# Bit-quantised feed-forward: which engine scales each tile, how the scales are made, and where tokens are rounded

## The chip, the core and the metric

The kernel runs on one core of a Trainium2 chip. A core has a matrix engine (TensorE, PE in the profile, with its weight loads as PEld), a vector engine (VectorE, DVE), an engine for activation functions (ScalarE, ACT), a general one (GpSimd, POOL) and a queue for transfers (SyncE, SP). Each runs its own list of instructions in order; semaphores tie them together. Matrix results land in PSUM, everything else lies in SBUF. The metric is the device time of one execution, in microseconds (us).

## The reference

Eight sequences of 256 tokens of width 256 pass through four pairs of attention and feed-forward, each added to its input. Only the last feed-forward is touched. It normalises each token, rounds tokens and weights to few levels, multiplies, convolves along the sequence, applies silu, rounds again and multiplies back:

```
def act_quant(x):
    scale = 127.0 / clip(max(abs(x), axis=-1), 1e-05)
    return clip(round(x * scale), -128, 127) / scale

h = bit_linear(x, w1)                       # 256 -> 1024
h = depthwise_conv1d(h, conv_w, conv_b)     # 3 taps along the tokens
h = silu(h)
out = bit_linear(h, w2)                     # 1024 -> 256
x = x + out
```

`bit_linear` applies `act_quant` to its input and multiplies by weights rounded to -1, 0, 1 times one scale.

## The kernel before

The program is a row of stages, one after the other; the last, `bit_ffn`, begins about 1534 us into the span and ends with it. It works on batches (sequences) of 256 tokens, held as two tiles of 128 tokens. The 1024 hidden channels are 8 channel tiles of 128 partitions by 256 tokens.

Every engine runs the same steps, 0 to 11; in step n five batches are in work, each in another phase (`new`, `turn`, `hid`, `end`, `last` for batches n, n-1, n-2, n-3, n-4):

- `new`: VectorE normalises the two token tiles (`xn`), finds each token's largest absolute value (`amax`, L2613) and makes two scales from it in four small operations (`token_scale`): `qs` = 127/max to round with, `qr` = max/127 to scale back. ScalarE rounds (`rounded`, L2718, into `q1`) by adding a large constant, `MAGIC`.
- `turn`: VectorE takes the constant off again and scales back (`unrounded`, L2632, into `q2`), TensorE turns the tokens (`turn_tokens`, into `px`), and they are split into a high part (ScalarE, L2725) and a low part (VectorE, L2637).
- `hid`: for each of 8 channel tiles TensorE makes the hidden values (`hidden`, L2808, one of three PSUM banks of `ph`), ScalarE does the middle tap with the bias (`middle_tap`, L2732), VectorE the first and the last tap (L2642, L2647), all into `y`. A bank is free again after the last tap, so the product of channel tile f waits for the last tap of tile f-3. After four channel tiles ScalarE applies silu to them (L2740, into `sT`).
- `end`: for each of two token tiles TensorE turns the activated values (`turn_silu`, L2819, into `pn`, one buffer), VectorE finds the largest of 1024 (L2656), makes two scales in four small operations (`tile_scale`: `saxc`, `srec`, `sqs`, `sqr`) and scales the tile (L2674, from `pn` into `s1`). GpSimd takes `MAGIC` off (`whole`, L2778, into `sq`), TensorE turns the tile back (`turn_back`, into `pb`).
- `last`: ScalarE copies `pb` out (`turned_back`, L2747, into `sqT`), TensorE multiplies (`product`, L2837, into `po`, one buffer), VectorE scales by `sqr` and adds to `x` (`residual`, L2681).

The order on each engine is written out by hand in its `step` function. On VectorE a step has 18 places, two per channel tile (even: first tap, odd: last tap) and two more, and other work is put in by place. On ScalarE and TensorE it goes by channel tile f. All waits are semaphores counted by batch. Steps 4 to 7 are a loop that holds two steps and runs twice; the other steps are written out. Steps 3 to 8 have all or nearly all phases in work and are called full here where all five are (4 to 7).

## Time and profile before

| | |
|---|---|
| median of 3 runs | 1703.01 us (1697.46 to 1704.25) |
| profiled execution, its own time | 1698.48 us |
| its span | 1696.6 us |
| granted TensorE clock, mean | 0.937 of full speed |
| busy share of the span | PE 86%, PEld 76%, DVE 57%, ACT 38%, POOL 25% |

The shares are means over all stages. This is the last part of the page's picture in 40 slices of 42.4 us each; the last four slices hold the stage that the change touches. Each digit is a tenth of the slice:

```profile
PE   4798997399986999999998799999999987875765
DVE  4576763312214666666665555555555547767996
ACT  1233333021213444444543244444444422234553
POOL 2011101134304443434332011010000026630212
```

Over the program TensorE is the busiest engine; in the last slices VectorE is. In a timeline row stand the start, the duration, engine, line, operation and what is written from what; a bracket gives the idle time before it and what ended it. The profile leaves out numbers in names: `f_q` is `q1` or `q2`, `f_s` is `s1`, `f_sq` is `sq`.

### The profile page before, as it was taken

Reading aid. Unit: us, or ns where it says so; the run is one execution under the profiler, and the core shown is the slowest. Engines: PE = TensorE matmul, PEld = TensorE weight load, DVE = VectorE, ACT = ScalarE, POOL = GpSimd, SP = SyncE. Lnnn points to the kernel's source line nnn. Section 1 sums busy time; section 2 is a strip of 40 time slices with the busy share of each in tenths; the row PEclk is TensorE's granted clock in tenths of the full one; section 3 lists DMA queues with packets and bytes.
Section 4 is the critical chain, followed back from the end, with each engine's and each line's share of the span. In section 5 each row is a group of like instructions: output and inputs, shape, how many; then the busy total and the mean of one; then the engine's idle time right before and its main releaser. Section 6 shows DMA issues by size and latency. Waiting matters only on the chain. (4 is left out here: it accounts for less than half of the span.)

```text
span 1696.6 us, 32771 instructions
## 1 busy us (share of the span) xinstructions
PE 1466.7 (86%) x11594; PEld 1282.5 (76%) x11594; DVE 971.6 (57%) x2432; ACT 638.5 (38%) x1414; POOL 420.6 (25%) x655
## 2 busy tenths in 40 slices
PE   4798997399986999999998799999999987875765
PEld 3466665389975788888887699999999976664554
DVE  4576763312214666666665555555555547767996
ACT  1233333021213444444543244444444422234553
POOL 2011101134304443434332011010000026630212
PEclk8699999599997999999999799999999999997898
DMA  7646430585410000010000444144338231100000
GB/s 149 114 79 112 77 52 14 203 277 180 133 41 29 8 8 20 14 36 20 1 8 14 165 171 157 41 174 175 120 109 294 69 94 47 35 7 1 14 12 26
DMA packets 97294, 139.83 MB, mean 82 GB/s; under 512 B 10080, under 2 KB 81248, under 8 KB 97056
## 3 DMA queue, kind: packets, MB, share of 16 engines
q1 hardware_dynamic: 79792, 109.83, 22.2%
q0 software_dynamic: 6368, 18.62, 3.9%
q10 hardware_dynamic: 11024, 9.97, 1.9%
q8 instruction: 63, 1.03, 0.3%
q14 instruction: 47, 0.39, 0.1%
HBM read 111.12 MB, written 14.42 MB: 74 GB/s over the span
## 5 line engine op out<-in xcount | busy, mean ns | idle before, releaser
L1872 PE MATMUL f_ph<-f_xgT,f_w 128*128 128x128 f32 x2496 | 287.0, 276 | 3.0 <-ACT f_xgT L1906 2.4
L1872 PEld LDWEIGHTS f_ph<-f_xgT,f_w 128*128 128x128 f32 x2496 | 283.8, 193 | 3.7 <-issue 1.9
L1031 ACT ACTIVATE a_work<-a_ps,a_bias 128x128 f32<-128x128 f32 (+1 forms) x256 | 104.1, 419 | 172.3 <-issue 90.7
L1953 DVE TENSOR_TENSOR f_w_low<-f_w,f_w_high 128x2048 fp32r<-128x2048 f32 x39 | 89.4, 2292 | 99.9 <-ACT f_w_high L1912 99.8
L1231 POOL TENSOR_TENSOR a_work<-a_work,a_recip 128x256 f32<-128x256 f32 (+1 forms) x128 | 103.2, 827 | 147.3 <-DVE a_recip L1150 146.3
L1843 POOL DMA_INDIRECT f_xg<-normed_x,order x38 | 36.0, 947 | 334.1 <-PE f_px L1861 325.6
L574 DVE CUSTOM_DVE_ANT_0 a_shut_s<-a_ps,a_neg 128x256 f32<-128x256 f32 x256 | 93.1, 420 | 41.5 <-PE a_ps L253 41.0
L486 ACT ACTIVATE a_pT<-a_ps 128x1024 f32<-128x1024 f32 x64 | 65.5, 1024 | 120.7 <-PE a_ps L253 120.7
L1912 ACT ACTIVATE f_w_high<-f_w 128x2048 fp32r<-128x2048 f32 x39 | 74.5, 1910 | 85.6 <-DVE f_yg L1965 85.6
L1155 DVE TENSOR_TENSOR a_qk<-a_ps,a_qk 128x512 fp32r<-128x512 f32 x64 | 44.3, 692 | 96.5 <-ACT a_qk L1048 96.5
L1674 PEld LDWEIGHTS f_ph<-f_xgT,f_w 128*128 128x128 f32 x736 | 87.8, 196 | 6.3 <-DMA f_w<-in_f_w 3.7
L1674 PE MATMUL f_ph<-f_xgT,f_w 128*128 128x128 f32 x736 | 88.9, 280 | 3.2 <-DMA f_w<-in_f_w 2.5
L1883 PE MATMUL f_py<-f_w_high,f_h_high 128*128 128x256 f32 x312 | 91.4, 293 | 0.0
L1883 PE MATMUL f_py<-f_w_high,f_h_low 128*128 128x256 f32 x312 | 88.1, 282 | 0.0
L1958 DVE TENSOR_TENSOR f_h_low<-f_raw,f_h_high 128x512 fp32r<-128x512 f32 x78 | 57.0, 730 | 54.3 <-ACT f_h_high L1916 54.3
L1883 PE MATMUL f_py<-f_w_low,f_h_high 128*128 128x256 f32 x312 | 88.0, 282 | 0.0
L1916 ACT ACTIVATE f_h_high<-f_raw 128x512 fp32r<-128x512 f32 x78 | 49.2, 631 | 91.8 <-DVE f_raw L1973 91.8
L1684 PE MATMUL f_py<-f_w,f_hT 128*128 128x256 f32 x368 | 83.5, 380 | 0.1
L1755 DVE TENSOR_SCALAR f_hT<-f_ph,f_b 128x128 f32<-128x128 f32 x92 | 25.9, 344 | 88.1 <-PE f_ph L1674 88.1
L1684 PEld LDWEIGHTS f_py<-f_w,f_hT 128*128 128x128 f32 x368 | 68.1, 190 | 9.1 <-issue 0.7
L1716 ACT ACTIVATE f_hT<-f_ph,f_b 128x128 f32<-128x128 f32 x92 | 26.2, 368 | 121.6 <-PE f_ph L1674 121.6
L1132 DVE TENSOR_REDUCE a_top_s<-a_ps 128x2 f32<-128x256 f32 (+1 forms) x128 | 64.2, 543 | 5.8 <-PE a_ps L917 5.8
(342 smaller groups left out, 3466.2 us busy)
## 6 DMA issues: line engine op xcount, KB each, us to landing
f_w<-in_f_w SPq DMA_DIRECT2D x70, 1024.0 KB, 7.3
sorted_y<-f_yg ACTq DMA_DIRECT2D x62, 128.0 KB, 1.7
a_qs<-a_part SPq DMA_DIRECT2D x48, 128.0 KB, 4.3
a_ks<-a_part SPq DMA_DIRECT2D x42, 128.0 KB, 6.2
normed_x<-a_xn SPq DMA_DIRECT2D x16, 256.0 KB, 2.2
x<-in_x SPq DMA_DIRECT2D x8, 256.0 KB, 6.6
a_mask<-in_mask SPq DMA_DIRECT2D x8, 256.0 KB, 6.4
a_maskT<-in_maskT SPq DMA_DIRECT2D x8, 256.0 KB, 6.5
```

The source lines that it names most:

```text
L486: act.activation(pT[:, u // 2 % 2, 2 * (u % 2):2 * (u % 2) + 2, :, :].rearrange("p j t n -> p j (t n)"), ps[:, ST:ST + 2, :], ACT.Exp, sca ...
L574: a = dve.tensor_tensor_reduce(out=shut_s[:, j, t, :], in0=ps[:, bank(m) + j, t * S:(t + 1) * S], in1=neg[:, m // U % 3, t, :], scale=1.0, ...
L1031: act.activation(prob[:, s, i, t * P:(P if t == 0 else TRI)], ps[:, SB + 2 * s + i, t * S:(t * S + P * (t + 1))], ACT.Exp, bias=bias[:, s, ...
L1132: dve.tensor_reduce(top_s[:, s, t, :], ps[:, SB + 2 * s:SB + 2 * s + 2, t * S:t * S + P * (t + 1)], AX.X, ALU.max).then_inc(max_done, 1)
L1231: pool.tensor_tensor(part, part, recip[:, s, t, :].unsqueeze(2).to_broadcast([P, 2, P * (t + 1)]), ALU.mult).then_inc(shares_done, 1)
L1674: mm = pe.matmul(ph[:, q, n, f * P:(f + 1) * P], w[:, s, k, (q * FQ + f) * P:(q * FQ + f + 1) * P], xgT[:, s, k, :], start=(k == 0), stop= ...
L1684: mm = pe.matmul(py[:, s, 0:D], hT[:, s, f, :], w2[:, s, f, :], start=(f == 0), stop=(f == FT - 1))
L1872: mm = pe.matmul(ph[:, q, n, f * P:(f + 1) * P], w[:, s, k, (q * FQ + f) * P:(q * FQ + f + 1) * P], xgT[:, s, k, :], start=(k == 0), stop= ...
L1883: mm = pe.matmul(py[:, s, 0:D], hT[a][:, s, f, :], w2_parts[b][:, s, f, :], start=(f == 0 and n == 0), stop=(f == FT - 1 and n == len(PASS ...
L1912: act.activation(w2_parts[0][:, s, :, :], w2[:, s, :, :], ACT.Copy).then_inc(w2_high, 1)
L1953: dve.tensor_tensor(w2_parts[1][:, s, :, :], w2[:, s, :, :], w2_parts[0][:, s, :, :], ALU.subtract).then_inc(w2_low, 1)
L1958: dve.tensor_tensor(hT[1][:, s, q * FQ:(q + 1) * FQ, :].rearrange("p f n -> p (f n)"), raw[:, q, :], hT[0][:, s, q * FQ:(q + 1) * FQ, :].r ...
```

## The change

Six edits, all in `bit_ffn`:

1. `token_scale` makes its two scales in two small operations: `qr` = max(amax, 1e-5) x 1/127 in one, `qs` = 1/`qr` in the next. The wait for `qr` in `unrounded` goes.
2. `tile_scale` likewise: `sunit` = max(sax, 1e-5) x 1/127, `sqs` = 1/`sunit`. The third, `sqr` = `sunit` x `unit` (the weights' scale), is made by GpSimd ahead of `whole`, with its own semaphore.
3. The first tile's scaling into `s1` is made by ScalarE (`scaled`), the second's by VectorE (`scaled_late`) at the end of the step.
4. ScalarE rounds the tokens after the middle tap of channel tile 7, ahead of the second silu, where it had done so at the step's end.
5. ScalarE's copy of the first turned tile (`turned_back`) moves from the end of a step to behind the middle tap 0 of the next; the copy of the second goes behind middle tap 3; the first silu goes behind middle tap 4.
6. TensorE's two products move from f = 2 and 4 to f = 4 and 5, VectorE's residuals from places 3 and 8 to 6 and 10.

The parts of the diff that carry these:

```diff
-                if k == 1:
-                    ins = dve.tensor_scalar(amaxc[:, :], amax[:, :], 1e-5, None, ALU.max)
-                if k == 2:
-                    ins = dve.reciprocal(rec[:, :], amaxc[:, :])
-                if k == 3:
-                    ins = dve.tensor_scalar(qs[:, :], rec[:, :], 127.0, None, ALU.mult)
-                if k == 4:
-                    ins = dve.tensor_scalar(qr[:, :], amaxc[:, :], 1.0 / 127.0, None, ALU.mult)
+                if k == 1:
+                    ins = dve.tensor_scalar(qr[:, :], amax[:, :], 1e-5, 1.0 / 127.0, ALU.max, ALU.mult)
+                if k == 2:
+                    ins = dve.reciprocal(qs[:, :], qr[:, :])
...
+            def scaled_late(pair, b):
+                i = TB * b + 1
+                dve.wait_ge(red_done, upto(pair, 3 * i + 2, 3 * TB))
+                if b >= 1:
+                    dve.wait_ge(sq_done, upto(pair, i - TB, TB))
+                dve.tensor_scalar(s1[:, 1, :], pn[:, :], sqs[:, 1:2], MAGIC, ALU.mult, ALU.add).then_inc(s1_done, 1)
...
+            def scaled(pair, b, t):
+                i = TB * b + t
+                act.wait_ge(red_done, upto(pair, 3 * i + 2, 3 * TB))
+                if i >= TB:
+                    act.wait_ge(sq_done, upto(pair, i - TB, TB))
+                act.activation(s1[:, t, :], pn[:, :], ACT.Identity, bias=magic[:, 0:1], scale=sqs[:, t:t + 1]
+                               ).then_inc(s1_done, 1)
...
+                pool.wait_ge(red_done, upto(pair, 3 * i + 1, 3 * TB))
+                if i >= TB:
+                    pool.wait_ge(resid_done, upto(pair, i - TB, TB))
+                pool.tensor_tensor(sqr[:, t:t + 1], sunit[:, t:t + 1], unit[:, 1:2], ALU.mult).then_inc(sqr_done, 1)
                 pool.wait_ge(s1_done, upto(pair, i, TB))
...
-                    if last and f == 2:
+                    if last and f == 4:
                         product(pair, n - 4, 0)
...
-                    if last and f == 4:
+                    if last and f == 5:
                         product(pair, n - 4, 1)
```

How the order moves is shown at three places; the names are as above, with the prefix `f3_`. First VectorE, the end of step 3, from the second tile's reduction to the next step. Before:

```order
L2656 TENSOR_REDUCE f3_sax<-f3_pn 128x1
L2619 RECIPROCAL f3_rec<-f3_amaxc 128x2
L2647 SCALAR_TENSOR_TENSOR f3_y<-f3_ph,t_cwu,f3_y 128x256
L2661 TENSOR_SCALAR f3_saxc<-f3_sax 128x1
L2642 SCALAR_TENSOR_TENSOR f3_y<-f3_ph,t_cwu,f3_y 128x256
L2663 RECIPROCAL f3_srec<-f3_saxc 128x1
L2621 TENSOR_SCALAR f3_qs<-f3_rec 128x2
L2647 SCALAR_TENSOR_TENSOR f3_y<-f3_ph,t_cwu,f3_y 128x256
L2665 TENSOR_SCALAR f3_sqs<-f3_srec 128x1
L2669 TENSOR_SCALAR f3_sqr<-f3_saxc,t_unit 128x1
L2623 TENSOR_SCALAR f3_qr<-f3_amaxc 128x2
L2674 TENSOR_SCALAR f3_s1<-f3_pn,f3_sqs 128x1024
```

And after:

```order
L2651 TENSOR_REDUCE f3_sax<-f3_pn 128x1
L2619 RECIPROCAL f3_qs<-f3_qr 128x2
L2642 SCALAR_TENSOR_TENSOR f3_y<-f3_ph,t_cwu,f3_y 128x256
L2658 TENSOR_SCALAR f3_sunit<-f3_sax 128x1
L2637 SCALAR_TENSOR_TENSOR f3_y<-f3_ph,t_cwu,f3_y 128x256
L2662 RECIPROCAL f3_sqs<-f3_sunit 128x1
L2642 SCALAR_TENSOR_TENSOR f3_y<-f3_ph,t_cwu,f3_y 128x256
L2669 TENSOR_SCALAR f3_s1<-f3_pn,f3_sqs 128x1024
```

Three small scalings between the last tap and the large scaling are gone, and so is one that stood ahead of the last tap; the scale `qs` for the tokens is ready two taps sooner. Taps are L2642 and L2647 before, L2637 and L2642 after.

Second ScalarE, all of step 3. Before:

```order
L2732 ACTIVATE f3_y<-f3_ph,t_fb,t_cwu 128x256 x4
L2725 ACTIVATE f3_xh<-f3_px 128x2x256
L2740 ACTIVATE f3_sT<-f3_y 128x1024
L2732 ACTIVATE f3_y<-f3_ph,t_fb,t_cwu 128x256 x4
L2740 ACTIVATE f3_sT<-f3_y 128x1024
L2747 ACTIVATE f3_sqT<-f3_pb 128x1024
L2718 ACTIVATE f3_q1<-f3_xn,f3_magic,f3_qs 128x256 x2
```

And after:

```order
L2728 ACTIVATE f3_y<-f3_ph,t_fb,t_cwu 128x256 x4
L2721 ACTIVATE f3_xh<-f3_px 128x2x256
L2728 ACTIVATE f3_y<-f3_ph,t_fb,t_cwu 128x256
L2743 ACTIVATE f3_s1<-f3_pn,f3_magic,f3_sqs 128x1024
L2736 ACTIVATE f3_sT<-f3_y 128x1024
L2728 ACTIVATE f3_y<-f3_ph,t_fb,t_cwu 128x256 x3
L2714 ACTIVATE f3_q1<-f3_xn,f3_magic,f3_qs 128x256 x2
L2736 ACTIVATE f3_sT<-f3_y 128x1024
```

The scaling (L2743) is new; one middle tap stands ahead of the first silu that stood behind it, and the rounding of the tokens stands ahead of the second silu.

Third TensorE, steps 10 and 11, the end of the program. Before:

```order
L2819 MATMUL f3_pn<-ident,f3_sT 128x128 x8
L2837 MATMUL f3_po<-t_w2q,f3_sqT 128x256 x8
L2828 MATMUL f3_pb<-identb,f3_sq 128x128 x8
L2837 MATMUL f3_po<-t_w2q,f3_sqT 128x256 x8
L2819 MATMUL f3_pn<-ident,f3_sT 128x128 x8
L2828 MATMUL f3_pb<-identb,f3_sq 128x128 x8
L2837 MATMUL f3_po<-t_w2q,f3_sqT 128x256 x8
L2828 MATMUL f3_pb<-identb,f3_sq 128x128 x8
L2837 MATMUL f3_po<-t_w2q,f3_sqT 128x256 x8
```

And after:

```order
L2831 MATMUL f3_pn<-ident,f3_sT 128x128 x8
L2840 MATMUL f3_pb<-identb,f3_sq 128x128 x8
L2849 MATMUL f3_po<-t_w2q,f3_sqT 128x256 x16
L2831 MATMUL f3_pn<-ident,f3_sT 128x128 x8
L2840 MATMUL f3_pb<-identb,f3_sq 128x128 x16
L2849 MATMUL f3_po<-t_w2q,f3_sqT 128x256 x16
```

The first tile's product stood between the turnings of the two tiles; now both turnings stand ahead of both products.

## Rows read from the trace of the kernel before

**Rows 1.** Stretch of step 6: us; busy PE, PEld, DVE, ACT, POOL; clock; DMA; GB/s.

```profile
1610.75:1627.77 17.02, 11.49 (x85) 9.73 (x83) 16.04 (x40) 9.28 (x16) 3.59 (x3) 0.90 0.04 15
```

**Rows 2.** Timeline of VectorE, last taps of steps 2, 3, 7, 9: start, duration.

```profile
1557.04 0.48 DVE L2647 SCALAR_TENSOR_TENSOR f_y<-f_ph,t_cwu,f_y 128x256 f32<-128x256 f32 x1
...
1572.44 0.47 DVE L2647 SCALAR_TENSOR_TENSOR f_y<-f_ph,t_cwu,f_y 128x256 f32<-128x256 f32 x1
...
1641.90 0.48 DVE L2647 SCALAR_TENSOR_TENSOR f_y<-f_ph,t_cwu,f_y 128x256 f32<-128x256 f32 x1
...
1672.63 0.48 DVE L2647 SCALAR_TENSOR_TENSOR f_y<-f_ph,t_cwu,f_y 128x256 f32<-128x256 f32 x1
```

**Rows 3.** Timeline of VectorE, around the start of step 6.

```profile
1607.94 0.14 DVE L2665 TENSOR_SCALAR f_sqs<-f_srec 128x1 f32<-128x1 f32 x1
...
1608.40 1.28 DVE L2674 TENSOR_SCALAR f_s<-f_pn,f_sqs 128x1024 f32<-128x1024 f32 x1
...
1610.75 1.05 DVE L2632 TENSOR_SCALAR f_q<-f_q,f_qr 128x256 f32<-128x256 f32 x1 [1.07 <-ACT f_q L2718]
...
1611.73 0.47 DVE L2642 SCALAR_TENSOR_TENSOR f_y<-f_ph,t_cwu,f_y 128x256 f32<-128x256 f32 x1
...
1612.12 0.34 DVE L2632 TENSOR_SCALAR f_q<-f_q,f_qr 128x256 f32<-128x256 f32 x1
...
1613.17 1.21 DVE L2656 TENSOR_REDUCE f_sax<-f_pn 128x1 f32<-128x1024 f32 x1
```

**Rows 4.** Timeline of ScalarE, around the start of step 6.

```profile
1608.06 1.06 ACT L2740 ACTIVATE f_sT<-f_y 128x1024 f32<-128x1024 f32 x1 [2.94 <-DVE f_y L2647]
...
1609.02 1.00 ACT L2747 ACTIVATE f_sqT<-f_pb 128x1024 bf16<-128x1024 bf16 x1
...
1609.92 1.08 ACT L2718 ACTIVATE f_q<-f_xn,f_magic,f_qs 128x256 f32<-128x256 f32 x2
...
1610.91 1.00 ACT L2732 ACTIVATE f_y<-f_ph,t_fb,t_cwu 128x256 f32<-128x256 f32 x2
```

**Rows 5.** Timeline of GpSimd, first tile of step 3 and second tile of step 5.

```profile
1567.66 1.90 POOL L2778 TENSOR_TENSOR f_sq<-f_s,f_magic 128x1024 bf16<-128x1024 f32 x1 [48.60 <-DVE f_s L2674]
...
1609.77 1.89 POOL L2778 TENSOR_TENSOR f_sq<-f_s,f_magic 128x1024 bf16<-128x1024 f32 x1 [5.40 <-DVE f_s L2674]
```

**Rows 6.** Timeline of VectorE, a small scaling in step 3.

```profile
1569.32 0.26 DVE L2617 TENSOR_SCALAR f_amaxc<-f_amax 128x2 f32<-128x2 f32 x1
```

**Rows 7.** Timeline of VectorE, tap 3 and tap 5 of step 6.

```profile
1616.43 0.47 DVE L2642 SCALAR_TENSOR_TENSOR f_y<-f_ph,t_cwu,f_y 128x256 f32<-128x256 f32 x1
...
1621.22 0.47 DVE L2642 SCALAR_TENSOR_TENSOR f_y<-f_ph,t_cwu,f_y 128x256 f32<-128x256 f32 x1
```

**Rows 8.** Timeline of ScalarE, the copy of turned tokens in step 6.

```profile
1616.14 0.60 ACT L2725 ACTIVATE f_xh<-f_px 128x512 fp32r<-128x512 f32 x1
```

**Rows 9.** Timeline of ScalarE, the table load in step 2.

```profile
1550.35 1.28 ACT L2740 ACT_TABLE_LOAD   x1
```

**Rows 10.** Timeline of VectorE, tap 4 and tap 5 of step 2.

```profile
1553.19 0.48 DVE L2642 SCALAR_TENSOR_TENSOR f_y<-f_ph,t_cwu,f_y 128x256 f32<-128x256 f32 x1 [1.51 <-ACT f_y L2732]
...
1554.70 0.48 DVE L2642 SCALAR_TENSOR_TENSOR f_y<-f_ph,t_cwu,f_y 128x256 f32<-128x256 f32 x1
```

**Rows 11.** Timeline of TensorE, turning of an activated tile, first and second of step 6.

```profile
1609.74 1.76 PE L2819 MATMUL f_pn<-ident,f_sT 128*128 128x128 f32 x8 [0.92 <-DVE f_s L2674]
...
1619.59 1.09 PE L2819 MATMUL f_pn<-ident,f_sT 128*128 128x128 f32 x8 [1.73 <-DVE f_s L2674]
```

**Rows 12.** Timeline of TensorE, the end of the program.

```profile
1687.60 1.03 PE L2828 MATMUL f_pb<-identb,f_sq 128*128 128x128 bf16 x8 [1.21 <-POOL f_sq L2778]
...
1689.74 1.89 PE L2837 MATMUL f_po<-t_w2q,f_sqT 128*128 128x256 bf16 x8 [1.12 <-ACT f_sqT L2747]
```

**Rows 13.** Timeline of VectorE, the last instruction.

```profile
1691.67 0.48 DVE L2681 SCALAR_TENSOR_TENSOR x<-f_po,f_sqr,x 128x256 f32<-128x256 f32 x1 [4.76 <-PE f_po L2837]
```

**Rows 14.** Timeline of GpSimd, a small product in an earlier stage.

```profile
1518.03 0.19 POOL L2137 TENSOR_TENSOR m_square<-m_guess 128x2 f32<-128x2 f32 x1
```

More of the change, by code:

```diff
@@ L2530, in bit_ffn @@
         xn, q1, q2 = (sb(n, [P, TB, D]) for n in ("xn", "q1", "q2"))
-        amax, amaxc, rec, qs, qr = (sb(n, [P, TB]) for n in ("amax", "amaxc", "rec", "qs", "qr"))
+        amax, qs, qr = (sb(n, [P, TB]) for n in ("amax", "qs", "qr"))
         xh, xl = (sb(n, [P, 2, DK, S + 2], F32R) for n in ("xh", "xl"))
@@ L2534, in bit_ffn @@
         sT = sb("sT", [P, 2, FT, S])
-        sax, saxc, srec, sqs, sqr = (sb(n, [P, TB]) for n in ("sax", "saxc", "srec", "sqs", "sqr"))
+        sax, sunit, sqs, sqr = (sb(n, [P, TB]) for n in ("sax", "sunit", "sqs", "sqr"))
         s1, sq = sb("s1", [P, TB, F]), sb("sq", [P, TB, F], BF16)
@@ L2630, in unrounded @@
                     dve.wait_ge(x_turned, upto(pair, b - 1))
-                dve.wait_ge(prep, upto(pair, 5 * b + 4, 5))
                 dve.tensor_scalar(q2[:, t, :], q1[:, t, :], MAGIC, qr[:, t:t + 1], ALU.subtract, ALU.mult
@@ L2686, in step @@
                 new, turn, hid, end, last = (is_batch(n - i) for i in range(5))
-                for place in range(2 * FT + 2):
+                for place in range(2 * FT + 1):
                     if turn and place < TB:
                         unrounded(pair, n - 1, place)
-                    if end and 3 <= place < 9:
+                    if end and 3 <= place < 6:
                         tile_scale(pair, n - 3, 0, place - 3)
@@ L2693, in step @@
                         (first_tap, last_tap)[place % 2](pair, n - 2, place // 2)
-                    if end and place >= 12:
+                    if end and 12 <= place < 15:
                         tile_scale(pair, n - 3, 1, place - 12)
-                    if last and place in (3, 8):
-                        residual(pair, n - 4, (3, 8).index(place))
+                    if end and place == 2 * FT:
+                        scaled_late(pair, n - 3)
+                    if last and place in (6, 10):
+                        residual(pair, n - 4, (6, 10).index(place))
                     if new and place in (5, 6):
@@ L2701, in step @@
                         low_part(pair, n - 1)
-                    if new and place in (9, 10, 12, 14, 16):
-                        token_scale(pair, n, (9, 10, 12, 14, 16).index(place))
+                    if new and place in (9, 10, 12):
+                        token_scale(pair, n, (9, 10, 12).index(place))
             every_step(dve, step)
@@ L2714, in rounded @@
                 for t in range(TB):
-                    act.wait_ge(prep, upto(pair, 5 * b + 3, 5))
+                    act.wait_ge(prep, upto(pair, 3 * b + 2, 3))
                     if b >= 1:
@@ L2751, in step @@
                 for f in range(FT):
+                    if hid:
+                        middle_tap(pair, n - 2, f)
+                    if last and f == 0:
+                        turned_back(pair, n - 4, 0)
                     if last and f == 3:
                         turned_back(pair, n - 4, 1)
-                    if hid:
-                        middle_tap(pair, n - 2, f)
                     if turn and f == 3:
                         high_part(pair, n - 1)
-                    if hid and f % 4 == 3:
-                        silu(pair, n - 2, f // 4)
-                    if end and f == 7:
-                        turned_back(pair, n - 3, 0)
-                if new:
-                    rounded(pair, n)
+                    if end and f == 4:
+                        scaled(pair, n - 3, 0)
+                    if hid and f == 4:
+                        silu(pair, n - 2, 0)
+                    if new and f == 7:
+                        rounded(pair, n)
+                    if hid and f == 7:
+                        silu(pair, n - 2, 1)
             every_step(act, step)
```

28 lines of the change are left out of this document (10 added, 18 removed).

## Prediction

> **What bounds the kernel now.** I read the view of stretches over the last stage first. In one full step (step 6) VectorE is busy 16.04 us of 17.02, TensorE 11.49 at a granted clock of 0.90, ScalarE 9.28, GpSimd 3.59 [rows 1]. So only in this stage, and in it only VectorE, is there no slack; the edits touch no other stage. Then I read VectorE's timeline to get the length of the steps, from the start of the last tap of one to that of the next: step 3 takes 15.40 us, steps 4 to 7 take 69.46 us (17.37 each), steps 8 and 9 together 30.73 us [rows 2]. Steps 10 and 11 are a chain that passes from engine to engine; the last instruction begins 19.04 us after the last tap of step 9 [rows 2, 13].
>
> Third, the start of a step. VectorE does three small scalings (0.46 us from the first to the large scaling), the large scaling `f_s` (1.28 us), waits 1.07 us for ScalarE's rounded tokens, and then its first `f_q` takes 1.05 us, where the same operation takes 0.34 us a little later [rows 3]. ScalarE is late with the tokens because it does silu and the copy of turned tiles first, 1608.06 to 1609.92 [rows 4]. The long `f_q` ends at 1611.80; GpSimd's `f_sq` ran from 1609.77 to 1611.66 [rows 3, 5]: VectorE was held until GpSimd was done.
>
> Of two neighbours on VectorE the second starts 0.08 us before the first one's end (1611.73 with 0.47, next 1612.12 [rows 3]). So a tap costs 0.39, a small scaling of 0.14 costs 0.06, the large scaling 1.19.
>
> **The change, part by part.**
>
> Start of a step, in us from where the three small scalings began (1607.94). Before, the next reduction starts at 5.23 [rows 3]. After, the small scalings are gone or stand earlier, so the large scaling runs 0 to 1.19 and its result is there at 1.28. The tokens are rounded already; the first `f_q` takes 0.26, to 1.45. The first tap needs ScalarE's bias tap, which now stands directly behind silu: silu from 0.12 (1608.06), the next 0.96 later (1609.02), bias tap about 0.56, so ready at 1.64 [rows 4]; tap 0 starts at 1.69. The second `f_q` would start at 2.08, but GpSimd's `f_sq` starts 0.09 after the large scaling (1609.77 against 1609.68), at 1.37, and runs 1.89, to 3.26 [rows 3, 5]. The `f_q` then frees VectorE at about 3.33. Two more taps: the reduction starts at 4.11. Gain 1.12. The hold is still there, it only moved from the first `f_q` to the second; without it the bias tap of channel tile 1 (behind the 1.00 us copy [rows 4], ready at 3.02) would be the limit and the reduction would start at 3.46, 0.65 earlier.
>
> The Trainium skill (SBUF — State Buffer, "SBUF: two separate sides") says that GpSimd and VectorE's two-port operations share a pair of ports as an exclusive lock: who starts first keeps it for the whole instruction. The trace agrees with the 1.05 against 0.34 us. The same page would count every `tensor_scalar` between SBUF tiles, the small ones too; that is the rival "held twice" below.
>
> Rest of a full step. The first tile's large scaling leaves VectorE: 1.19. Two small scalings of that tile and one of the tokens go: 0.06 to 0.13 each, 0.2 together. Gain 1.4. What it costs ScalarE: no row shows this scaling there; by the nearest rows it is 1.06 (silu, same size [rows 4]) to 1.28 (VectorE's own [rows 3]); I take 1.15, nearer the ScalarE row. ScalarE has 17.0 - 9.3 = 7.7 us free [rows 1], so the total is no problem, but the place is: between bias tap 3 and bias tap 5 ScalarE now has the copy 1.00, the token copy 0.60 [rows 8], two bias taps of 0.56, the scaling 1.15 and silu 1.06, less five overlaps of 0.1: 4.4 us. VectorE needs from tap 3 to tap 5 4.79 us now [rows 7], less 1.19 and a small one: 3.5 us. ScalarE's lead at tap 3, 0.7 to 1.3 us by my schedule, covers most. I put the wait at 0.3 us per step (bounds 0 and 1.0).
>
> GpSimd gets one product of one column per tile, 0.19 us by a row of another stage [rows 14]. It stands ahead of `f_sq` and waits for the residual of the same buffer. The residual comes at place 6 of a step, before ScalarE's scaling ends, so in full steps it costs nothing; behind it waits only `f_sq`, and TensorE's turn back at the step's end, over 3 us later.
>
> TensorE's two products move two and one places back, behind the turn back of the second tile. Tap 3 needs the hidden product 3, which stands behind the turned tokens (held `f_q`, 3.4) and the turn back of a tile that GpSimd ends at 3.26; both are needed anyway. Cost 0 in full steps. At half clock TensorE's group takes 1.76 instead of 1.09 [rows 11]; that is inside the 0.3.
>
> So a full step saves 1.12 + 1.4 - 0.3 = 2.2 us; four of them 8.8.
>
> Step 3: no `f_sq` runs at its start. The two roundings (1.08, less 0.1 [rows 4]) no longer stand ahead of bias tap 0: 0.9; rest as above 1.4. Together 2.3.
>
> Steps 8 and 9: step 8 starts like a full step (1.1), step 9 rounds no tokens and gains only the small scalings (0.5); the rest 1.4 each. VectorE has no norms and fewer other things between tap 3 and tap 5 here, so it waits more for ScalarE: 0.6 each. Together 3.2.
>
> Steps 0 to 2: in step 2 silu's table load of 1.28 us [rows 9] stood ahead of bias tap 4, and VectorE waited 1.51 us; tap 5 started at 1554.70 [rows 10]. Now the load comes behind bias tap 4 (ScalarE free from about 1550.70): load to 1551.98, silu to 1552.95, bias tap 5 ready 1553.5. Gain 1.1. Two small operations less in the tokens' chain of steps 0 and 1: 0.3. Together 1.4.
>
> Steps 10 and 11: at the end TensorE turned the last tile back (1687.60, 1.03 us), waited for ScalarE's copy, did one product (1.89) and the residual followed at 1691.67 [rows 12, 13], 3.04 us after the turning. Now both products stand behind this turning, and the second one waits for the first one's residual: 1.89 + 0.48 + 1.89 and three hand-overs of 0.1: 4.5 us. Loss 1.5. Against it stand two dependent small operations less for each of two tiles (0.2 each, 0.8) and the earlier start of the step (0.4). Net loss 0.3.
>
> Sum: -1.4 - 2.3 - 8.8 - 3.2 + 0.3 = -15.4 us. The profiled execution took 1698.48 us (span 1696.6), so it would take 1683.1; it lies 4.5 under the median of the runs, 1703.01. Off the median: 1687.6. I forecast 1687.5.
>
> **The rivals.**
>
> Everything meets: no wait for ScalarE (0.3 x 4 and 0.6 x 2 back), tail even, and the hold falls away in part because GpSimd's new small product delays `f_sq` past the second `f_q` (0.65 x 5). That is 2.4 + 0.3 + 3.2 = 5.9 more: 1681.5. Against it: the small product's inputs are ready long before, so it delays nothing.
>
> Held twice: at the loop's ends VectorE may reach the first `f_q` after GpSimd's start, and the tokens' small scaling at place 10 may meet the first tile's `f_sq`. A small scaling took 0.26 us at 1569.32, to 1569.58, where `f_sq` ended at 1569.56 [rows 5, 6], so small ones are held too. By my schedule `f_sq` of the first tile ends 0.8 us before that place; with ScalarE a microsecond late it doesn't, and up to 1.3 us per step in six steps go: 7.8. Time 1695.5.
>
> Nothing comes of it: another wait fills what VectorE gives up, ScalarE's queue above all. At its upper bound (1.0 per full step instead of 0.3, and 2 in steps 8 and 9) plus held twice: about 3 + 3 + 7.8 back of 15.4: 1701.5.
>
> Slower, by TensorE's clock: if the moved waits keep it at its lower level (1.2 GHz) through the steps, its 11.49 us [rows 1] grow by the 1.76 / 1.09 of rows 11 to 18.5, and with the 0.9 us in which it waits for the large scaling [rows 11] a step takes 19.4, 2.0 more than the 17.37. It then bounds the stage: 5 steps, +10, time 1713. It decides once more than about three quarters of each step run at the lower level. Against it: 0.90 was granted, and in a shorter step its gaps shrink.
>
> **How the numbers follow.** Under 0.5% (8.5 us) is what a measurement of this kernel can't tell from no change. Forecast 0.60 (own range 1683 to 1692), everything meets 0.12, held twice 0.18, nothing 0.07, slower 0.03. The range leaves out the last two and little of the others: 1677 to 1697. Faster (below 1694.5): 0.60 + 0.12 + two thirds of 0.18 = 0.84; same: a third of 0.18 and the 0.07 = 0.13; slower 0.03.
>
> **What would show it.** The distance of last taps in full steps near 15.1 us; no wait of VectorE for `f_q`; a second, not a first, `f_q` of 1.2 us or more; the new ScalarE scaling 1.06 to 1.28 us; tap 5 of a full step waiting 0 to 0.5 us for ScalarE; step 2 without the 1.51 us wait at tap 4; some 4.5 us between the last turn back and the last residual. Wrong: VectorE waiting over 1 us per step for bias taps, small scalings of 0.3 us or more at place 10, or a granted clock well under 0.9 in full steps.

## The result, and the profile after

| | before | after |
|---|---|---|
| median, run side by side on one chip | 1701.48 us (1697.46 to 1704.78) | 1683.70 us (1677.31 to 1688.16) |
| ratio, after to before | | 0.9905, 95% interval 0.9882 to 0.9928 |
| profiled execution, its own time | 1698.48 us | 1677.31 us |
| its span | 1696.6 us | 1675.4 us |
| granted TensorE clock, mean | 0.937 | 0.945 |

Faster by 0.95%, 17.8 us between the medians. 1687.5 was forecast, with 1677 to 1697 as the range. Of the 21.2 us between the spans, 4.5 are not the change: the stage's first instruction starts at 1534.26 us before and at 1529.74 after, and nothing ahead of it was edited (in the kernels of the experiments below, whose earlier stages are the same too, it lies between 1528.90 and 1543.99). From there to the start of the last residual the stage took 157.41 us and takes 140.69: 16.7 less, where the prediction's sum was 15.4. "Stage" below is always this stretch, which leaves out what the rest of the program does.

The view of stretches over steps 4 to 7, each from the start of the last tap of one step to that of the next (length, then busy time of PE, PEld, DVE, ACT, POOL, then granted clock, share of the DMA engines' time, GB/s), first two of the four of before:

```profile
1572.44:1589.97 17.53, 12.87 (x85) 10.90 (x84) 16.07 (x43) 9.39 (x15) 3.79 (x2) 0.79 0.05 16
...
1624.68:1641.90 17.22, 11.50 (x86) 9.85 (x85) 16.24 (x42) 9.39 (x15) 3.79 (x2) 0.90 0.05 15
```

and of after:

```profile
1564.07:1578.81 14.74, 11.15 (x85) 10.06 (x84) 14.58 (x34) 10.43 (x17) 4.31 (x4) 0.86 0.06 19
1578.81:1593.56 14.75, 11.13 (x87) 9.95 (x87) 14.59 (x35) 10.53 (x17) 4.24 (x4) 0.90 0.06 19
1593.56:1608.67 15.11, 11.56 (x86) 10.20 (x85) 14.66 (x34) 10.49 (x17) 4.31 (x4) 0.89 0.05 18
1608.67:1623.42 14.75, 10.95 (x86) 9.88 (x85) 14.59 (x35) 10.51 (x17) 4.24 (x4) 0.88 0.05 18
```

VectorE is still the engine without slack (14.59 of 14.75), ScalarE took over a scaling of 1.2 us per step, and the steps lie near the 15.1 that was forecast.

The start of step 5 after, which answers to [rows 3 to 5]. VectorE:

```profile
1579.21 1.27 DVE L2669 TENSOR_SCALAR f_s<-f_pn,f_sqs 128x1024 f32<-128x1024 f32 x1
1580.41 0.34 DVE L2627 TENSOR_SCALAR f_q<-f_q,f_qr 128x256 f32<-128x256 f32 x1
1580.88 0.48 DVE L2637 SCALAR_TENSOR_TENSOR f_y<-f_ph,t_cwu,f_y 128x256 f32<-128x256 f32 x1
1581.28 1.37 DVE L2627 TENSOR_SCALAR f_q<-f_q,f_qr 128x256 f32<-128x256 f32 x1
...
1583.36 1.21 DVE L2651 TENSOR_REDUCE f_sax<-f_pn 128x1 f32<-128x1024 f32 x1
```

GpSimd and then ScalarE (its first copy, and later in the step the new scaling):

```profile
1580.57 1.93 POOL L2790 TENSOR_TENSOR f_sq<-f_s,f_magic 128x1024 bf16<-128x1024 f32 x1 [1.83 <-DVE f_s L2669]
```

```profile
1580.75 1.01 ACT L2751 ACTIVATE f_sqT<-f_pb 128x1024 bf16<-128x1024 bf16 x1
...
1586.68 1.23 ACT L2743 ACTIVATE f_s<-f_pn,f_magic,f_sqs 128x1024 f32<-128x1024 f32 x1
```

The first `f_q` is short and nothing waits for it; the second is held: it ends at 1582.65, just behind the end of `f_sq` at 1582.50. The hold moved from one to the other, as forecast. The wait of 1.51 us at tap 4 of step 2 [rows 10] is gone; what is left there is this, at tap 5:

```profile
1548.67 0.48 DVE L2637 SCALAR_TENSOR_TENSOR f_y<-f_ph,t_cwu,f_y 128x256 f32<-128x256 f32 x1 [0.47 <-ACT f_y L2728]
```

The end of the program, which answers to [rows 12, 13]. TensorE, then VectorE's last residual:

```profile
1665.12 1.03 PE L2840 MATMUL f_pb<-identb,f_sq 128*128 128x128 bf16 x8 [3.83 <-POOL f_sq L2790]
1665.94 1.91 PE L2849 MATMUL f_po<-t_w2q,f_sqT 128*128 128x256 bf16 x8
1668.53 1.87 PE L2849 MATMUL f_po<-t_w2q,f_sqT 128*128 128x256 bf16 x8 [0.67 <-DVE x L2675]
```

```profile
1670.43 0.48 DVE L2675 SCALAR_TENSOR_TENSOR x<-f_po,f_sqr,x 128x256 f32<-128x256 f32 x1 [2.05 <-PE f_po L2849]
```

From the end of the last turning back (1666.15) to the last residual it is 4.28 us, where 4.5 was forecast and it was 3.04 before.

### The profile page after: what moved, and what is told of

The parts are those of the page before. It is cut to its first block and busy times, and to the rows that moved or that the text cites. A ratio compares the mean times of both kernels' runs of the same rounds, so it can differ in the third digit from the quotient of the medians.

```text
span 1675.4 us, 32751 instructions
## 1 busy us (share of the span) xinstructions
PE 1453.5 (87%) x11594; PEld 1275.4 (76%) x11594; DVE 960.2 (57%) x2376; ACT 648.3 (39%) x1422; POOL 424.8 (25%) x671
```

## The experiments

Twelve kernels ran. A ratio is always to the kernel before, and has an interval of 3 to 6 us on each side, so most of what is said of parts rests on the stage and on single steps of one profiled execution each. All times are us; the clock of a step is the mean that the view of stretches shows for it.

| kernel | ratio (interval) | stage | steps 0-2 | 3 | 4-7 | 8 | 9 | rest |
|---|---|---|---|---|---|---|---|---|
| before | 1 | 157.41 | 22.78 | 15.40 | 69.46 | 16.35 | 14.38 | 19.04 |
| after | .9905 (.9882-.9928) | 140.69 | 21.27 | 13.06 | 59.35 | 14.18 | 14.14 | 18.69 |
| 1 scaling back on VectorE | .9929 (.9904-.9953) | 147.41 | 21.16 | 14.81 | 63.73 | 14.84 | 13.83 | 19.04 |
| 2 rounding behind silu | .9922 (.9905-.9938) | 144.28 | 21.31 | 13.96 | 61.43 | 14.81 | 14.14 | 18.63 |
| 3 four small operations | .9918 (.9896-.9940) | 149.38 | 21.01 | 13.61 | 63.58 | 15.97 | 15.57 | 19.64 |
| 4 unroundings ahead | .9936 (.9916-.9956) | 148.18 | 20.83 | 13.12 | 64.97 | 16.47 | 14.15 | 18.64 |
| 5 unroundings back to back | .9917 (.9884-.9950) | 143.52 | 20.83 | 13.12 | 62.35 | 14.55 | 13.33 | 19.34 |
| 6 late copy | .9883 (.9856-.9911) | 141.29 | 21.31 | 13.13 | 59.43 | 14.34 | 14.74 | 18.34 |
| 7 ahead and late copy | .9906 (.9870-.9941) | 140.90 | 20.81 | 13.13 | 60.90 | 14.13 | 13.63 | 18.30 |
| 8 both products back | .9969 (.9947-.9992) | 152.79 | 21.31 | 13.12 | 67.43 | 16.89 | 16.54 | 17.50 |
| 9 first product early at the end | .9904 (.9882-.9927) | 142.43 | 21.13 | 13.00 | 60.58 | 14.78 | 13.36 | 19.58 |
| 10 first product back | .9935 (.9912-.9958) | 146.27 | 21.30 | 13.06 | 62.66 | 16.38 | 14.17 | 18.70 |
| 11 unroundings around the scaling | .9898 (.9874-.9921) | 142.13 | 20.83 | 13.13 | 60.45 | 15.33 | 13.66 | 18.73 |
| 12 = 11 + 6 + 9 | .9889 (.9862-.9915) | 136.49 | 20.83 | 13.13 | 58.73 | 13.92 | 13.63 | 16.25 |

**1. The first tile's scaling back on VectorE.**

```diff
+                    if end and place == 8:
+                        scaled_first(pair, n - 3)
...
-                    if end and f == 4:
-                        scaled(pair, n - 3, 0)
```

The added lines are VectorE's, the ones taken out ScalarE's.

> The changed kernel with one edit undone: the first tile's scaling stands on VectorE again, at place 8 of a step (where it was before), not on ScalarE. Measured on the stage alone, from its first instruction (the memset of the constant) to the start of the last residual: 157.41 us before, 140.69 us after. Theory (VectorE's queue is the bound, each microsecond taken from it is gained): the scaling comes back as 1.19 us in each of steps 3 to 9, 8.3 us, less the waits for ScalarE that the changed kernel has in steps 6, 8 and 9 (0.3, 0.7 and 2.4 us, of which half goes): stage about 147 us, ratio to before about 0.994. Rival (ScalarE's copy was paid in ScalarE's queue, so moving it back costs nothing): stage within 1 us of 140.7.

Stage 147.41. All four full steps took 15.93 or 15.94 at a clock of 0.88 to 0.90, 1.18 more than the 14.75 of after, which is the 1.19 that the scaling costs in VectorE's queue. The step that answers to [rows 1]:

```profile
1586.39:1602.32 15.93, 11.44 (x87) 9.96 (x86) 15.77 (x36) 9.52 (x16) 4.24 (x4) 0.90 0.05 18
```

**2. The rounding behind the second silu again.**

```diff
-                    if new and f == 7:
-                        rounded(pair, n)
                     if hid and f == 7:
                         silu(pair, n - 2, 1)
+                    if new and f == 7:
+                        rounded(pair, n)
```

> The changed kernel with one edit undone: ScalarE rounds the tokens at the end of a step again, behind the second silu. Theory (the rounding is needed for the first unrounding, and it delays the bias tap 0 behind it, but most of that is hidden because GpSimd holds VectorE anyway): the first unrounding, not the second, is held until GpSimd's work ends (over 1 us), and the first reduction of a full step starts 0.5 to 0.9 us later; over steps 3 to 8 the stage becomes 4 to 5 us longer, 145 us. Rival (the whole wait of 1 us and the held time of 1 us come back beside each other, 2 us a step): 151 us or more.

Full steps of 15.35 or 15.36, 0.61 more than in after. The hold and the wait are on the first `f_q` again, as before the change:

```profile
1607.38 1.59 DVE L2627 TENSOR_SCALAR f_q<-f_q,f_qr 128x256 f32<-128x256 f32 x1 [0.53 <-ACT f_q L2714]
```

**3. Four small operations per scale, none on GpSimd.**

```diff
-                    ins = dve.tensor_scalar(qr[:, :], amax[:, :], 1e-5, 1.0 / 127.0, ALU.max, ALU.mult)
-                if k == 2:
-                    ins = dve.reciprocal(qs[:, :], qr[:, :])
+                    ins = dve.tensor_scalar(amaxc[:, :], amax[:, :], 1e-5, None, ALU.max)
+                if k == 2:
+                    ins = dve.reciprocal(rec[:, :], amaxc[:, :])
...
```

Two more operations follow, and `tile_scale` is undone likewise.

> The changed kernel with the small operations undone: four small operations for each scale on VectorE as before (the third scale also on VectorE, none on GpSimd), all else as changed. Theory: five small operations more in a full step at 0.06 to 0.13 us, of which two or three stand bare between last tap and large scaling where each costs 0.15: 0.6 to 0.7 us a step, and 0.4 us in each dependent chain of steps 0, 1, 10 and 11: stage 140.7 + 4.5 + 1.6 = 146.8 us. Rival (small operations vanish in the gaps between taps that wait for each other anyway): stage below 142.5 us.

149.38, 2.6 over what was expected. The stretches tell the two parts apart:

```profile
1592.09:1608.38 16.29, 12.76 (x86) 11.32 (x85) 15.64 (x41) 10.37 (x17) 3.79 (x2) 0.79 0.06 18
...
1624.79:1640.15 15.36, 11.06 (x85) 9.99 (x85) 15.29 (x41) 10.39 (x17) 3.79 (x2) 0.89 0.05 17
```

The two steps at a clock of 0.89 take 15.52 and 15.36, 0.6 to 0.8 over after: the small operations. The two at 0.79 take 0.9 more, with 1.5 us more of busy TensorE. In full steps the small operations are worth what was said; that the rest is TensorE at its lower level more of the time is read from these rows, and no run isolates it. In steps 0 and 1 they cost the 0.4 too (12.20 us from the start of the stage to tap 0 of step 2, against 11.79 in after), but step 2 was 0.67 shorter than in after, so the column of steps 0 to 2 doesn't show it.

**4. Both unroundings ahead of the late scaling,** so that neither meets `f_sq`.

```diff
-                    if turn and place < TB:
-                        unrounded(pair, n - 1, place)
...
+                    if new and place == 2 * FT:
+                        for t in range(TB):
+                            unrounded(pair, n, t)
                     if end and place == 2 * FT:
                         scaled_late(pair, n - 3)
```

> The changed kernel with the two unroundings of a step's tokens moved from places 0 and 1 of the next step to ahead of the late large scaling, so that they are done before GpSimd starts on that tile. Theory (an operation of VectorE between SBUF tiles is held while GpSimd computes, 1.37 us instead of 0.34 in steps 4 to 8): both take 0.34 us, the large scaling comes 0.5 us later, tap 0 follows it at once, and the reduction is then bound by TensorE's turning of the tile: a full step gets 0.5 to 1.1 us shorter, the stage 3 to 5 us, 136 to 138 us. Rival (the long duration is something of the instruction itself or of its input's arrival, not of GpSimd): the second unrounding stays long wherever it stands, stage 140 us or more.

A miss, by 10 to 12 us. The hold was gone (both unroundings together took 0.61), and VectorE's busy time fell to 13.93 per step, but the steps grew:

```profile
1587.77:1603.33 15.56, 11.40 (x86) 10.10 (x85) 13.93 (x34) 10.50 (x17) 4.21 (x4) 0.89 0.06 18
1603.33:1619.58 16.25, 12.73 (x86) 11.20 (x85) 13.94 (x35) 10.51 (x17) 4.27 (x4) 0.79 0.05 17
```

The late scaling started 0.93 after the last tap instead of 0.40, and TensorE waited for it:

```profile
1590.12 1.94 PE L2832 MATMUL f_pn<-ident,f_sT 128*128 128x128 f32 x8 [1.06 <-DVE f_s L2669]
```

From this came a new theory. Beside VectorE's queue runs a second chain: late scaling, turning of the next tile, hidden products 2 and 3 with the turned tokens and a turn back between, middle taps, copies, ScalarE's scaling, silu, middle tap 5. In the changed kernel it is nearly as long as the queue.

**5. Both unroundings back to back behind the late scaling.**

```diff
-                    if turn and place < TB:
-                        unrounded(pair, n - 1, place)
+                    if turn and place == 0:
+                        for t in range(TB):
+                            unrounded(pair, n - 1, t)
```

> The changed kernel with the two unroundings standing one behind the other at place 0, directly behind the late large scaling; before, tap 0 stood between them. It asks who gets the way to SBUF that VectorE and GpSimd hold against each other. GpSimd's work starts 0.17 us after the first unrounding, the second would start 0.26 after it. Theory (it goes to who asks first, and GpSimd asks between the two): the second is held, 1.4 us as now, but ahead of tap 0, which then can't use the time; the first reduction of a full step starts 0.3 to 0.4 us later, the stage is 142 to 143 us. Rival (VectorE keeps it while its next operation wants it too): both take 0.34, VectorE gets 1 us free per full step, of which the chain through ScalarE lets some 0.3 through: 138 to 139.5 us.

Stage 143.52, 0.5 over what was expected, and one of the four full steps took 16.56 where the others took 15.26; the hold stays. The two, now one row, took 2.25 us, to 1590.05; `f_sq` had begun 0.16 after the first of them and ended at 1589.89. VectorE, then GpSimd:

```profile
1587.80 2.25 DVE L2627 TENSOR_SCALAR f_q<-f_q,f_qr 128x256 f32<-128x256 f32 x2
```

```profile
1587.96 1.93 POOL L2791 TENSOR_TENSOR f_sq<-f_s,f_magic 128x1024 bf16<-128x1024 f32 x1 [1.84 <-DVE f_s L2669]
```

Being next in VectorE's queue doesn't keep the port: GpSimd takes it between two neighbours.

**6. ScalarE's second copy out of the second chain.**

```diff
-                    if last and f == 3:
+                    if last and f == 5:
                         turned_back(pair, n - 4, 1)
...
-                    if last and f == 5:
+                    if last and f == 7:
                         product(pair, n - 4, 1)
...
-                    if last and place in (6, 10):
+                    if last and place in (6, 15):
```

> The changed kernel with ScalarE's copy of the second turned tile moved from behind bias tap 3 to behind bias tap 5, its product from f = 5 to 7, its residual from place 10 to 15. That takes 0.9 us out of the chain late scaling, turning of the tile, hidden products 2 and 3, bias tap 3, copies, bias tap 4, scaling, silu, bias tap 5. Theory (in the changed kernel VectorE's queue is the bound and this chain is slack by 0 to 0.5 us in steps 4, 5 and 7): only the waits at tap 5 go (0.3 in step 6, 0.7 in step 8, 1.5 in step 9): stage 138 to 139.5 us. Rival (the chain is the bound already): 0.9 us in each of steps 4 to 8, stage 135 us or less.

Full steps as in after (59.43 against 59.35), so in the changed kernel VectorE's queue is the longer one, and the gain looked for in steps 8 and 9 didn't come: a miss in size.

**7. Experiments 4 and 6 together.**

> Both moves together: the unroundings ahead of the late scaling (stage 148.2 us by itself, 7.5 more than the changed kernel, although nothing is held) and ScalarE's second copy behind bias tap 5. Theory (the first move made the chain that begins with the late scaling 0.5 us later and so the bound; the trace shows VectorE waiting at taps 3 and 5): with 0.9 us out of the chain the loss goes and the gain of the free unroundings shows: full steps of 14.2 to 14.8 us, stage 136 to 140 us. Rival (moving the unroundings costs by itself, by TensorE's clock or by the tokens' turning): stage 146 us or more also with the second move.

Stage 140.90, near the 136 to 140 of the theory, where 4 alone had 148.18. But the steps don't bear the theory out at like clock: at 0.79 a full step took 16.32 (in 4: 16.25 to 16.61), at 0.89 it took 15.79 (in 4: 15.56), with VectorE waiting 1.12 us at tap 3. The gain lies in the two full steps at a clock of 1.00, and experiment 4 has none of those. Steps 4, 5 and 7 of experiment 7 (step 4 has no transfers out yet and one instruction of GpSimd less):

```profile
1562.84:1579.16 16.32, 12.66 (x86) 11.17 (x85) 13.76 (x33) 10.51 (x17) 4.07 (x3) 0.79 0.01 2
1579.16:1593.44 14.28, 9.96 (x86) 8.60 (x85) 13.84 (x35) 10.30 (x16) 4.24 (x4) 1.00 0.06 20
...
1607.95:1623.74 15.79, 11.37 (x86) 10.12 (x85) 13.99 (x34) 10.48 (x17) 4.24 (x4) 0.89 0.05 17
```

So it isn't shown that the late copy by itself makes up for the later start; what is shown is that with it the loss is gone in the steps in which TensorE kept its upper level. The late copy may bring that about: the three kernels that have it (6, 7, 12) ran 6 of their 12 full steps at 1.00, the other eleven 1 of 44. Each is a single profiled execution, and why it is so stays open. Open is also the size in experiment 4: at like clock (0.89 against 0.90) its step is 0.8 us longer than in after, for a start only 0.53 later, while the turning took 1.94 us instead of 1.55.

**8. Both products and residuals where they stood before** (edit 6 alone undone).

```diff
-                    if last and f == 4:
+                    if last and f == 2:
                         product(pair, n - 4, 0)
...
-                    if last and f == 5:
+                    if last and f == 4:
                         product(pair, n - 4, 1)
...
-                    if last and place in (6, 10):
+                    if last and place in (3, 8):
```

> The changed kernel with TensorE's products back at f = 2 and 4 and VectorE's residuals at places 3 and 8. Theory: in steps 10 and 11 the first product stands between the two turnings again, so from the last turning to the last residual it takes 3.0 us instead of 5.3: 1.5 to 2.3 us less; in full steps the first product stands ahead of hidden product 2 and 3, in the chain that is nearly the bound, at up to 1.6 us: it adds 0.3 to 1 us to each of steps 4 to 9. Stage 141 to 145 us. Rival (products are free wherever they stand): 138.5 to 139.2 us, only the end changes.

The tail fell by 1.2, where 1.5 to 2.3 was expected. The full steps grew by 2.0 each instead of 0.3 to 1, a miss of nearly 8 us in the stage, and it is the slowest version: ratio 0.9969. Of the 16.7 us only 4.6 are left without edit 6. The clock isn't it (0.90 in all four full steps; two of them):

```profile
1565.47:1582.08 16.61, 11.43 (x86) 9.80 (x85) 14.76 (x35) 10.54 (x17) 4.20 (x4) 0.90 0.05 17
1582.08:1599.00 16.92, 11.41 (x87) 9.83 (x85) 14.90 (x34) 10.67 (x17) 4.20 (x4) 0.90 0.05 17
```

TensorE waits for ScalarE's copy ahead of the second product, with hidden product 4 queued behind it, and VectorE then waits for middle tap 4:

```profile
1589.19 0.56 ACT L2728 ACTIVATE f_y<-f_ph,t_fb,t_cwu 128x256 f32<-128x256 f32 x1 [0.84 <-PE f_ph L2820]
1589.65 1.01 ACT L2751 ACTIVATE f_sqT<-f_pb 128x1024 bf16<-128x1024 bf16 x1
```

```profile
1590.72 1.05 PE L2849 MATMUL f_po<-t_w2q,f_sqT 128*128 128x256 bf16 x8 [1.57 <-ACT f_sqT L2751]
```

```profile
1592.96 0.48 DVE L2637 SCALAR_TENSOR_TENSOR f_y<-f_ph,t_cwu,f_y 128x256 f32<-128x256 f32 x1 [1.08 <-ACT f_y L2728]
```

This isn't the order of the kernel before. There ScalarE's copy stood ahead of middle tap 3, and edit 5 moved it behind; TensorE then waited 0.58 us for it, and VectorE nowhere for middle tap 4 (step 6 of before, ScalarE and TensorE):

```profile
1614.78 1.02 ACT L2747 ACTIVATE f_sqT<-f_pb 128x1024 bf16<-128x1024 bf16 x1 [0.32 <-PE f_pb L2828]
1615.70 0.56 ACT L2732 ACTIVATE f_y<-f_ph,t_fb,t_cwu 128x256 f32<-128x256 f32 x1
```

```profile
1615.86 1.05 PE L2837 MATMUL f_po<-t_w2q,f_sqT 128*128 128x256 bf16 x8 [0.58 <-ACT f_sqT L2747]
```

So experiment 8 shows what the products' old places cost beside the copies' new ones. No run has both old, and how the 2.0 us divide between the later copy and the shorter queue of VectorE stays open.

**9. The first product at f = 2 in steps 10 and 11 alone.**

```diff
-                    if last and f == 4:
+                    if last and f == (4 if hid else 2):
                         product(pair, n - 4, 0)
```

> The changed kernel, with TensorE's product of the first tile at f = 2 again in the steps without a hidden phase (10 and 11) and nothing else. Theory: at the end of the program the first product and its residual then run while GpSimd still has the last tile, so one product (1.89 us) and one residual fewer stand behind the last turning back: tail 18.69 -> 17.5 us (the run with both products moved back showed 17.50), every step before it unchanged, stage 140.7 -> 139.5. Rival: the residual's hand-over, not the product, sets the end; then the tail stays within 0.3 of 18.7.

A miss: 19.58 instead of 17.5. From the end of the last turning back to the last residual it is 3.05 again instead of 4.28, as said. But in step 10 the product, 1.91 at TensorE's lower level, now stands ahead of a turning back, its copy and the turning of the next tile; from one turning of a tile to the next it took 7.30 us (1662.70 to 1670.00) instead of 5.52 (1653.56 to 1659.08). The order isn't all of it: experiment 8 has TensorE's same order in steps 10 and 11 and took 17.50 there, at a clock of 0.86 and with residuals at earlier places; this one had 0.69, and after 0.73. Up to step 9 this kernel issues what after does, and still one step took 1.3 us more:

```profile
1586.90:1601.64 14.74, 9.90 (x86) 8.65 (x85) 14.58 (x34) 10.50 (x17) 4.24 (x4) 1.00 0.06 19
...
1616.70:1632.74 16.04, 12.81 (x86) 11.36 (x85) 14.78 (x34) 10.50 (x17) 4.24 (x4) 0.79 0.05 16
```

In the long step TensorE turned the first tile in 1.94 us and the tokens in 1.06, and VectorE then waited 0.45 at tap 3 and 0.65 at tap 5; in the one at 1.00 the turnings took 1.06 and 0.66 and VectorE waited nowhere. The mean alone doesn't tell: step 4 of this kernel, at 0.88, took 14.74 too; its first turning was slow (1.97), but the tokens' was not (0.60). That is the grain of every comparison of stages here: one such step is 1.3 us.

**10. Only the first product and its residual back** (f = 2, place 3), the second left at f = 5.

> Half of the earlier run that moved both products back (stage 152.79): here only the first tile's product stands at f = 2 and its residual at place 3, as before the change; the second tile's stay where the change put them (f = 5, place 10). Theory: what costs 2 us per full step is the second product at f = 4, because TensorE waits there for ScalarE's copy behind middle tap 3 with the hidden product of channel tile 4 queued behind it; the first product at f = 2 costs nothing since middle taps 2 and 3 have 1.2 to 1.7 us of lead. Full steps 14.8 (steps 4 to 7: 59 to 60), tail 17.5, stage 139 to 141. Rival: the first product, ahead of the hidden product of channel tile 2 and 1.05 to 1.6 us long, is what costs; then full steps stay at 16 to 17 and the stage at 148 or more.

Neither theory holds alone: 62.66 in steps 4 to 7, between 59.35 and 67.43. Moving the first product back costs 3.3 of the 8.1, moving the second as well adds 4.8. ScalarE's bias tap 2 came 5.92 us after the last tap (after: 3.89), since at the lower level the product stands 1.91 us ahead of hidden product 2:

```profile
1587.89 1.91 PE L2849 MATMUL f_po<-t_w2q,f_sqT 128*128 128x256 bf16 x8
```

**11. The unroundings around the late scaling,** one ahead, one behind.

```diff
+                    if new and place == 2 * FT:
+                        unrounded(pair, n, 0)
                     if end and place == 2 * FT:
                         scaled_late(pair, n - 3)
+                    if new and place == 2 * FT:
+                        unrounded(pair, n, 1)
```

> The changed kernel with VectorE's two unroundings around the late scaling: the first ahead of it, the second directly behind it. Theory (hold and second chain): the late scaling is 0.26 us later, not 0.53 as with both ahead, and the second unrounding asks for the port 0.09 us before GpSimd's f_sq can, so neither is held (0.34 us each) and f_sq starts some 0.15 later. VectorE's reduction starts 3.8 us after the last tap instead of 4.55; of these 0.7 the ScalarE lead at middle taps 4 and 5 gives back 0.2 to 0.6. Full steps 14.2 to 14.8, stage 137 to 140. Rival: 0.26 us of delay to the second chain costs as the 0.53 did (7.5 us for both ahead); then full steps are 15.2 or more and the stage 143 or more.

Both are short now, the second since it starts first (1594.93 against 1595.09 for `f_sq`):

```profile
1593.47 0.34 DVE L2627 TENSOR_SCALAR f_q<-f_q,f_qr 128x256 f32<-128x256 f32 x1
1593.73 1.28 DVE L2669 TENSOR_SCALAR f_s<-f_pn,f_sqs 128x1024 f32<-128x1024 f32 x1
1594.93 0.34 DVE L2627 TENSOR_SCALAR f_q<-f_q,f_qr 128x256 f32<-128x256 f32 x1
...
1601.00 0.48 DVE L2637 SCALAR_TENSOR_TENSOR f_y<-f_ph,t_cwu,f_y 128x256 f32<-128x256 f32 x1 [0.96 <-ACT f_y L2730]
```

Yet the stage is 142.13, neither the gain nor the rival's loss: full steps of 15.12, 16.08 (at 0.79), 14.90 and 14.35. What VectorE was given, it spends waiting for middle taps: in every full step 0.32 at tap 1 and 0.2 to 0.7 at tap 5, and 0.96 at tap 3 of this one.

**12. The three together: 11, the late copy of 6, the early product of 9.**

> The three together that should each help or be neutral: unroundings around the late scaling, ScalarE's second copy behind middle tap 5 with its product at f = 7 and residual at place 15, and the first product at f = 2 in steps 10 and 11. Theory: the copy's 0.9 us leave the second chain, so nothing gives back the 0.7 us of the hold: full steps 13.9 to 14.3, steps 4 to 7 56 to 57.5, tail 17.5, stage 134.5 to 138, total about 1678. Rival: something else in VectorE's queue or TensorE's clock (which sat at 0.79 in the first full step of the version with both ahead and late copy) takes it back: stage 139 or more.

Stage 136.49, 4.2 under after and inside what was expected, though steps 4 to 7 (58.73) stay over their 56 to 57.5; two full steps ran at a clock of 1.00:

```profile
1585.60:1599.67 14.07, 9.99 (x86) 8.60 (x85) 13.72 (x35) 10.31 (x16) 4.29 (x4) 1.00 0.06 20
...
1613.96:1629.54 15.58, 11.40 (x86) 10.14 (x85) 14.02 (x34) 10.50 (x17) 4.28 (x4) 0.89 0.05 17
```

Of the 4.2, 2.4 are at the end: with the second product behind the turning of the next tile (f = 7), TensorE gets from turning to turning in 4.00. But it also ran these steps at a clock of 0.93, where after had 0.73 (the first turning took 1.06, not 1.94), so the 2.4 isn't the order's alone. In the medians it isn't told from after: 0.9889 (0.9862 to 0.9915) against 0.9905 (0.9882 to 0.9928).

## Why the prediction was right, and where it was not

| term | forecast | measured |
|---|---|---|
| steps 0 to 2 | -1.4 | -1.51 |
| step 3 | -2.3 | -2.34 |
| steps 4 to 7 | -8.8 | -10.11 |
| steps 8 and 9 | -3.2 | -2.41 |
| steps 10 and 11 | +0.3 | -0.35 |
| sum | -15.4 | -16.72 |

The forecast of 1687.5 lay 3.8 over the median of 1683.70. Of these, 1.3 are the sum. Another 1.5 are the base, 1703.01 in the three runs of the forecast and 1701.48 in the six of the comparison, and about 1 is what the medians moved beyond the stage (17.8 against 16.7).

**Steps 0 to 2.** Of the 1.51, 0.42 lie ahead of tap 0 of step 2 (forecast 0.3, the small operations) and 1.09 in step 2 (forecast 1.1, the table load).

**The start of a step.** The reduction follows 4.55 us after the last tap; by the schedule of the prediction it was 0.40 + 4.11 = 4.51. The moved hold is shown by the long second `f_q` in after, by its absence in 11, and by its being on the first in 2. The Trainium skill (SBUF — State Buffer, "SBUF: two separate sides") has the two engines' port as an exclusive lock kept for a whole instruction. The 1.37 us against 0.34 agree, and so does experiment 5, where `f_sq` came between the two. In experiment 11 `f_sq` is recorded as starting while the second `f_q` still ran (to 1595.27), and it took 1.93 us as in after, so the record doesn't show that GpSimd waited then.

**Where the chances went.** "Held twice" did not occur: the small scaling of tokens took 0.16 and the hold is on one `f_q`. In step 5 `f_sq` of the first tile ended at 1589.88 and that scaling began at 1590.55, so the two didn't meet, by 0.7 us where the prediction had 0.8. "Everything meets" was right in that ScalarE made VectorE wait 0, 0, 0.29 and 0 us at tap 5 of the full steps instead of 0.3 each; the hold did not fall away.

**Steps 4 to 7.** The mechanism was right, the size short by 1.3 us. Two things made it short, by 1.7 together, and the edits themselves gave some 0.4 less than their sum. 0.9 is the wait of 0.3 per step, which came in one step. Another 0.8 is in the base: the four steps of before were not alike, two ran at a clock of 0.79 and 0.82 and took 17.53 and 17.58, two at 0.90 and took 17.13 and 17.22, and the prediction subtracted from their mean. After has none of the slow kind. The experiments price the edits in steps at like clock: the scaling 1.18 (forecast 1.19), the small operations 0.6 to 0.8 and the earlier rounding 0.61. These two are together 1.2 to 1.4, where the forecast had 1.12 at the start of the step and 0.2 in the rest.

**The step that was wrong in its reason.** "Cost 0 in full steps" for TensorE's moved products. The move costs nothing, but it is not neutral either: without it, experiment 8 gives back 12.1 of the 16.7 us. The sum came out since it was made for all six edits together, with VectorE as the only bound; that is in part luck, for the prediction never asked what the other edits would bring with the old order of products. There TensorE's wait for the copy, 0.58 us before, becomes 1.57 and makes middle tap 4 late. The copy had moved (edit 5) and the steps were some 2.4 us shorter than before; which of the two made the old places harmful no run tells.

**Steps 8 and 9.** Step 8 gave 2.17 (forecast 1.1 + 1.4 - 0.6 = 1.9), step 9 only 0.24 (forecast 0.5 + 1.4 - 0.6 = 1.3). In step 9 two terms were mis-sized: VectorE's busy time fell by 1.46 (12.99 to 11.53) where 0.5 + 1.4 was forecast, and its waits for ScalarE grew by 1.2, not 0.6, from 1.24 us to 0.39 + 0.36 + 0.19 + 1.49 = 2.4, the last at tap 5:

```profile
1648.07 0.48 DVE L2637 SCALAR_TENSOR_TENSOR f_y<-f_ph,t_cwu,f_y 128x256 f32<-128x256 f32 x1 [1.49 <-ACT f_y L2728]
```

Step 9 had a clock of 1.00 before and 0.88 after, but the same instructions took 13.36 us at 0.87 in experiment 9, against 14.14 here, so the mean clock doesn't explain it; how much is TensorE's stays open.

**The end.** The loss at the last turning back was 1.24 (forecast 1.5), the gains beside it 1.6 (forecast 1.2). Right in kind, and the sign turned on 0.6 us, less than the 2.1 by which these steps differ between experiments 8 and 9, with the same order on TensorE.

**The slower rival,** TensorE's clock: the granted clock in full steps was 0.86 to 0.90, so it did not come; but experiments 3 and 9 show that it is a real cost in this kernel: 0.9 and 1.3 us for a step at 0.79, where before the change it was 0.4 (17.5 against 17.2). It is also why stages that differ by less than 1.3 us aren't told apart above, and why those of experiments 4 and 7 can't be compared without the clock of their steps.

## What to carry to other kernels

When the engine that bounds is relieved, take the next longest chain and write it out as carefully as the first: here it was close behind, and the later savings on VectorE (0.7 us a step in experiment 4, 0.7 in 11) went into waits along it. Before two versions are compared, compare their steps at the same clock. An edit priced at nothing should also be asked what the others are worth without it. A hold between two engines is avoided by who starts first, and not by who stands next in a queue.
